# An LSTM with routed experts on one core: the first batch routed group by group, the first expert rows turned inside the last LSTM step, and scatters at most two in flight

## The reference

```python
g = xp_t + h_prev @ u                       # 512 x 512 gates, 8 steps in sequence
c = sigmoid(f) * c_prev + sigmoid(i) * tanh(cand);  h = sigmoid(o) * tanh(c)
x = layernorm(x + hs)
logits = einsum('GSM,ME->GSE', x, router_w)          # G=8 groups, S=512, M=128, E=8
# top 2 experts of a token; place p in its expert by cumulated count; kept where p < C
expert_inputs = einsum('GSEC,GSM->EGCM', dispatch, x)          # C = 128 slots
hidden = gelu(expert_inputs @ w0) * (expert_inputs @ w1)       # H = 688
out = einsum('EGCM,GSEC->GSM', hidden @ wo, combine)
y = layernorm(x + out)
```

## Time and profile before

| | |
|---|---|
| timed, median of 3 | 306.52 us |
| the profiled execution, first to last instruction | 342.1 us |
| TensorE / VectorE / ScalarE / GpSimd busy | 293.1 / 251.6 / 217.3 / 186.6 us |
| mean granted clock of TensorE | 0.921 |

### The profile page before, as it was taken

The page is one execution under the profiler, slowest core; times in us unless marked ns, Lnnn a source line. Parts: engine busy times, 40 slices in busy tenths (PEclk is TensorE's granted clock), DMA queues, the critical chain, the costliest instruction groups (busy, mean ns, idle before and its releaser), DMA issues.

```text
span 342.1 us, 5646 instructions
## 1 busy us (share of the span) xinstructions
PE 293.1 (86%) x1692; PEld 244.8 (72%) x1692; DVE 251.6 (74%) x794; ACT 217.3 (64%) x495; POOL 186.6 (55%) x153
## 2 busy tenths in 40 slices
PE   8999999697754695529999999999999999998880
PEld 6666665496744695419999987877888888888770
DVE  2789989599621585026888889889877776996985
ACT  4689887665720473026777876877765566566884
POOL 5012788887777027787773433437436536559500
PEclk9999999999885598557999999999999999999996
DMA  6996582486521015324443326344214227325265
GB/s 218 363 407 167 127 251 74 99 229 191 166 89 57 22 28 151 97 35 47 49 62 57 52 46 175 76 113 64 47 16 63 33 19 134 65 36 86 24 163 153
DMA packets 46685, 37.20 MB, mean 109 GB/s; under 512 B 7057, under 2 KB 40784, under 8 KB 46656
## 3 DMA queue, kind: packets, MB, share of 16 engines
q1 hardware_dynamic: 35392, 26.56, 26.1%
q0 software_dynamic: 11264, 10.29, 19.6%
HBM read 17.86 MB, written 17.10 MB: 102 GB/s over the span
## 4 chain that ended last, share of the span: by engine, by line
PE 67%; DVE 10%; issue 7%; ACT 6%; another core or an unknown queue 5%; POOL 3%; DMA 1%; SPq 0%; ACTq 0%; DVEq 0%
PE big L647 11%; PE big L645 11%; PE big L646 10%; PE big L552 6%; PE b_ht L664 3%; PE b_xnt L661 2%; PE b_xnt L664 2%; PE b_xnt L662 2%; PE b_ht L661 2%; PE b_ht L662 2%; PE big L538 2%; POOL tokens L494 2%; PE b_rt L681 2%; PE big L539 2%
## 5 line engine op out<-in xcount | busy, mean ns | idle before, releaser
L834 ACT ACTIVATE act_g<-big 128x256 f32<-128x256 f32 (+1 forms) x144 | 65.0, 452 | 90.8 <-PE big L647 59.6
L645 PE MATMUL big<-x_hi,e_hi 128*128 128x256 f32 (+1 forms) x264 | 89.5, 339 | 0.3 <-issue 0.3
L647 PE MATMUL big<-x_lo,e_hi 128*128 128x256 f32 (+1 forms) x264 | 86.9, 329 | 1.3 <-issue 1.3
L646 PE MATMUL big<-x_hi,e_lo 128*128 128x256 f32 (+1 forms) x264 | 86.9, 329 | 1.0 <-issue 1.0
L479 POOL DMA_INDIRECT slots<-rows,slot_ix x64 | 68.5, 1071 | 33.6 <-issue 18.5
L494 POOL DMA_INDIRECT tokens<-contrib,token_ix x32 | 51.4, 1607 | 42.2 <-DVE token_ix L1108 34.4
L494 POOL DMA_INDIRECT tokens<-zero_rows,token_ix x28 | 45.2, 1614 | 35.5 <-DVE token_ix L1108 27.5
L646 PEld LDWEIGHTS big<-x_hi,e_lo 128*128 128x128 f32 x264 | 52.9, 200 | 4.5 <-issue 1.1
L647 PEld LDWEIGHTS big<-x_lo,e_hi 128*128 128x128 f32 x264 | 52.7, 199 | 4.4 <-issue 0.4
L645 PEld LDWEIGHTS big<-x_hi,e_hi 128*128 128x128 f32 x264 | 53.0, 201 | 3.7 <-issue 0.2
L1116 DVE TENSOR_TENSOR term_i<-act_g,big 128x256 f32<-128x256 f32 (+3 forms) x36 | 18.3, 508 | 17.4 <-ACT act_g L834 12.0
(11 more groups left out here) (204 smaller groups left out, 672.9 us busy)
## 6 DMA issues: line engine op xcount, KB each, us to landing
e_raw<-in_L_ffn_w_kernel_dram SPq DMA_DIRECT2D x16, 320.0 KB
slots<-zero_rows SPq DMA_DIRECT2D x8, 548.0 KB, 7.6
e_raw<-in_L_ffn_wo_kernel_dram SPq DMA_DIRECT2D x8, 320.0 KB
xd<-slots SPq DMA_DIRECT2D x16, 137.0 KB
xd<-slots SPq DMA_DIRECT2D x8, 274.0 KB
e_lo<-e_raw POOLq DMA_DIRECT2D x4, 544.0 KB
x<-in_L_attn_input_seq_dram SPq DMA_DIRECT2D x8, 256.0 KB, 4.5
tokens<-rows SPq DMA_DIRECT2D x8, 256.0 KB
```

The source lines that it names most:

```text
L645: pe.matmul(dst, e_hi[q][:, c0:c0 + m], xdt_hi[u % 2][:, 0:w], start=True, stop=False)
L646: pe.matmul(dst, e_lo[q][:, c0:c0 + m], xdt_hi[u % 2][:, 0:w], start=False, stop=False)
L647: mm = pe.matmul(dst, e_hi[q][:, c0:c0 + m], xdt_lo[u % 2][:, 0:w], start=False, stop=True)
L834: nc.scalar.activation(act0[n % RH][0:m, 0:w], pre(n, P)[0], ACT.Gelu_apprx_tanh).then_inc(gelu_ready, 1)
```

## The change

- Batch 0 is routed as two parts, group 0 in step 2 and group 1 in step 3, each with four tiles. There are five parts r instead of four; batch 1 is routed in step 5 as before, batches 2 and 3 are parts 3 and 4. Every routing function takes a part and works on its tiles.
- GpSimd does power(0), power(1) and low_half(0,0) and then the scatters; power(2) to power(7) and three low_halfs are placed among the tiles anew: power(5) ahead of batch 1's third tile.
- From batch 2 on, each scatter from the second tile waits until the same choice's scatter of the tile before has landed (one semaphore for each choice). `load_xd` waits for both semaphores.
- `turn_xd(0)` stands behind `h_part(7)` and ahead of `turn_sum(6)`; `high_xd(0)` behind step 7's gates; on VectorE shift(5), scale_less(3), low_xd(0), stat, moment and variance of group 6 stand ahead of h of step 7. Both `keep_warm` blocks are gone.
- In units 0 and 1 turn_sum(7), places(3), logits(7), the normalizing of groups 5 to 7 and the routing of batch 2 are placed anew.

```diff
-    LOWS_AMONG = {(1, 0): (1, 0), (1, 1): (1, 1)}
-    ROOTS_AMONG = {(0, 2): 3, (0, 5): 4, (1, 0): 5, (1, 2): 6, (1, 3): 7}
+    LOWS_AMONG = {(0, 6): (0, 1), (1, 0): (1, 0), (1, 1): (1, 1)}
+    ROOTS_AMONG = {(0, 3): 2, (0, 5): 3, (0, 7): 4, (1, 2): 5, (1, 4): 6, (1, 5): 7}
+    ROUTED_IN = {2: 0, 3: 1, 5: 2}
+        def batch_of(r):
+            return max(r - 1, 0)
+        def groups_of(r):
+            return range(r, r + 1) if r < GB else range(GB * (r - 1), GB * r)
+        def tiles_of(r):
+            return slice(r * T, (r + 1) * T) if r < GB else slice(0, BT)
...
             def load_xd(u):
...
-                    sp.wait_ge(routed[b], 16 * 2 * BT)
+                    for c in range(2):
+                        sp.wait_ge(routed[b][c], 16 * BT)
...
                     for c in range(2):
+                        if b >= NB // 2 and t:
+                            pool.wait_ge(routed[b][c], 16 * t)
                         pool.indirect_dma_start(
                             slots, bass.IndirectOffsetOnAxis(ap=slot_ix[b][:, 2 * t + c:2 * t + c + 1], axis=0),
-                            rows[:, b * BT + t, :], None, bounds_check=slot_bound, oob_is_err=False).then_inc(routed[b], 16)
+                            rows[:, b * BT + t, :], None, bounds_check=slot_bound, oob_is_err=False).then_inc(routed[b][c], 16)
...
-            for s in range(3):
-                if s == 2:
-                    low_half(0, 0)
+            for s in range(2):
                 power(s)
-            low_half(0, 1)
-            for b in range(NB):
-                scatter(b, range(BT))
+            low_half(0, 0)
+            for r in range(NR):
+                scatter(r)
...
             for s in range(1, S):
                 h_part(s)
+                if s == S - 1:
+                    turn_xd(0)
                 turn_sum(s - 1)
...
-                if s >= 3 and s % 2 == 1 and s < S - 1:
-                    places(s // 2 - 1)
-            pe.wait_ge(gate_read, gate_no(S - 1, 2))
-            keep_warm(8, big[2])
-            turn_xd(0)
-            turn_sum(S - 1)
-            keep_warm(8, big[2])
+                if s in ROUTED_IN:
+                    places(ROUTED_IN[s])
...
+                    if (u, k) == (0, 3):
+                        turn_sum(S - 1)
+                    elif (u, k) == (0, 4):
+                        places(NR - 2)
+                    elif (u, k) == (0, 5):
+                        logits(S - 1)
...
+                if s == S - 1:
+                    shift(S - 3)
+                    scale_less(NR - 2)
+                    low_xd(0)
+                    stat(S - 2, range(T))
+                    moment(S - 2)
+                    variance(S - 2)
                 dve.wait_ge(tanh_ready, s + 1)
...
-            stat(S - 2, range(T))
-            moment(S - 2)
-            variance(S - 2)
-            shift(S - 3)
-            scale_less(NB - 2)
-            low_xd(0)
             for n in range(5):
-                gate_step(NB - 2, n)
-            slot_base(NB - 2)
-            void_base(NB - 2)
+                gate_step(NR - 2, n)
+            chunk(0, 0)
+            slot_base(NR - 2)
+            void_base(NR - 2)
+            chunk(0, 1)
+            shift(S - 2)
+            low_weights(2, 0)
+            chunk(0, 2)
...
```

More of the change, by code:

```diff
@@ L204, in build @@
         gate_rows_in = sem("gate_rows_in")
-        routed = [sem(f"routed{b}") for b in range(NB)]
+        routed = [[sem(f"routed{b}_{c}") for c in range(2)] for b in range(NB)]
         raw_in = [sem(f"raw_in{q}") for q in range(2)]
@@ L341, in b_xd @@
         def b_xd(u):
[L343 removed]
+            return b_xt
         def piece(n):
@@ L466, in low_half, with scatter @@
                 pool.dma_start(e_lo[e][:, cols], e_raw[e % 2][:, cols], accum_op=ALU.add).then_inc(elo_in[e], 16)
-            def scatter(b, tiles):
+            def scatter(r):
+                b = batch_of(r)
                 pool.wait_ge(zeros_out[b], 16 * GB)
-                pool.wait_ge(slot_step, AS * (b + 1))
-                pool.wait_ge(gate_rows_in, b + 1)
-                for t in tiles:
+                pool.wait_ge(slot_step, AS * (r + 1))
+                pool.wait_ge(gate_rows_in, r + 1)
+                for t in range(tiles_of(r).start, tiles_of(r).stop):
                     if (b, t) in ROOTS_AMONG:
@@ L569, in logits, with places @@
                 mm.then_inc(logits_ready, 1)
[L571 to L575, removed]
+            def places(r):
+                pe.wait_ge(chosen_ready, r + 1)
+                for g in groups_of(r):
+                    lo, pl = g % GB * T, place_ps(batch_of(r))[:, g % GB]
                     pe.matmul(pl[:, 0:T, :, :], before[:, :], chosen[:, lo:lo + T, :, :], start=True, stop=True)
@@ L743, in negative_weights, with exp @@
                 nc.scalar.activation(e_lo[e][:, piece(n)], e_hi[e][:, piece(n)], ACT.Copy, scale=-1.0).then_inc(negative_ready[e], 1)
[L745 to L747 removed]
+            def exp(r):
+                act.wait_ge(scaled, r + 1)
+                nc.scalar.activation(ex[:, tiles_of(r), :], less[:, tiles_of(r), :], ACT.Exp).then_inc(exp_ready, 1)
             def norm_rows(s, tiles):
@@ L765, in _ @@
                         high_x(1)
-                if s >= 3 and s % 2 == 1 and s < S - 1:
-                    exp(s // 2 - 1)
+                if s in ROUTED_IN:
+                    exp(ROUTED_IN[s])
+                if s == S - 1:
+                    high_xd(0)
                 for x in HIGH_X_AHEAD.get(s, []):
@@ L949, in best, with scale_less @@
                                   ALU.subtract).then_inc(less_ready, 1)
[L951 to L960, removed]
+            def scale_less(r):
+                gs, ts = groups_of(r), tiles_of(r)
+                dve.wait_ge(less_ready, gs.stop)
+                dve.wait_ge(power_ready, gs.stop)
+                view = less[:, ts, :].rearrange("p (g t) e -> p g t e", t=T)
+                q0 = gs.start % GB
+                dve.tensor_tensor(view, view, root_y[:, q0:q0 + len(gs), 0:T].unsqueeze(3).broadcast_to([P, len(gs), T, E]), ALU.mult).then_inc(scaled, 1)
@@ L1001, in assign_batch @@
                 else:
-                    dve.wait_ge(slot_step, AS * b + n)
+                    dve.wait_ge(slot_step, AS * r + n)
                 if n == 1:
-                    for g in range(GB):
+                    for g in range(gs.start, gs.stop):
                         ins = dve.tensor_tensor(place[:, g * T:(g + 1) * T, :, :], place_ps(b)[:, g, 0:T, :, :],
@@ L1186, in _ @@
             variance(S - 1)
+            chunk(0, 3)
+            assign(NR - 2, 0)
+            assign(NR - 2, 1)
             best(S - 2)
-            shift(S - 2)
-            low_weights(2, 0)
-            chunk(0, 0)
-            assign_batch(NB - 2, 0)
-            assign_batch(NB - 2, 1)
-            chunk(0, 1)
-            assign_batch(NB - 2, 2)
-            assign_batch(NB - 2, 3)
-            chunk(0, 2)
-            shift(S - 1)
-            assign_batch(NB - 2, 4)
-            assign_batch(NB - 2, 5)
-            chunk(0, 3)
-            low_weights(2, 1)
-            gate_values(NB - 2)
-            gate_row(NB - 2)
-            chunk(0, 4)
-            best(S - 1)
+            low_weights(2, 1)
+            chunk(0, 4)
+            shift(S - 1)
+            assign(NR - 2, 2)
+            assign(NR - 2, 3)
             chunk(0, 5)
             low_weights(2, 2)
-            for k in range(3):
-                chunk(1, k)
-            scale_less(NB - 1)
+            assign(NR - 2, 4)
+            assign(NR - 2, 5)
+            chunk(1, 0)
+            gate_values(NR - 2)
+            gate_row(NR - 2)
+            chunk(1, 1)
+            best(S - 1)
+            chunk(1, 2)
+            scale_less(NR - 1)
             low_weights(2, 3)
```

148 lines of the change are left out of this document (78 added, 70 removed).

## The result

The changed kernel takes 312.59 us (median of 4 runs, 311.99 to 315.27) against 306.38 us before: a ratio of 1.0226, 95% interval 1.018 to 1.0272, or 6.2 us slower. The forecast was 306.1 us, its range ended at 309.5. Medians in this document are of all runs, while a ratio and its interval leave out runs over 1.5% above the fastest of their kernel, so that a ratio need not be the quotient of the two medians beside it. The profiled execution is one of the timed ones, with a span of 310.2 us and 1.8 us around it.

What follows compares the result with a forecast made beforehand. TensorE paces the LSTM and the units from 3 on, VectorE the boundary. Sum: 306.52 - 0.3 (routing to boundary) + 0 (idle matmuls) + 0 (limit) - 0.1 (stalls) = 306.1 us; own range 305.2 to 307.2, 8 in 10 302.6 to 309.5.

Steps and rivals of the forecast that it cites:

- (b): GpSimd: first scatters near 30.1 us, xd(0) issued near 59.9, so TensorE's 2.10 us wait for the first gathered rows goes.
- the stalls of units 3 and 5: Expert units of 24.25 and 25.30 us against 6.30: 37.0 us excess, read as mostly made by profiling.
- the stall-free sum: Whole timed execution read as the profile without its stalls: span near 305.1 us (342.1 - 37.0) and 1.4 us outside.
- (a): Routing by groups in LSTM steps 2 and 3: 2.5 us more VectorE work, LSTM slip 1.6 us, bounds 0 and 2.9.
- (c): Boundary of LSTM and experts: VectorE gaps filled, new power(5) wait; net -0.96 to +0.64 us at unit 1's third chunk.
- the prediction's high bound: Start of unit 0 at half clock without the idle matmuls: +1.7 us at most, 0 taken.
- (d): Two scatters in flight: 8 us more on GpSimd, at most 12.8; +0 on time, bounds 0 and +4; stall relief -0.1.
- Who waits: Behind the limited scatters only the adds, which TensorE needs in unit 9: late by 0 to 1.5 us, 4 at most.
- the rivals: Stalls relieved, about 304.0 us (0.24); throttle makes unit 9 late, about 309.0 (0.17); boundary loses, 307.7 (0.14).

Runs made afterwards that it cites:

- e1: Changed kernel with low_half(0,1) ahead of tile 2 of batch 0 instead of tile 6: 306.86 us against 306.49 before, ratio 0.9993.
- e3: Changed kernel without the limit of two scatters in flight in batches 2 and 3: 313.03 us, ratio to before 1.022.
- e4: Changed kernel with low_half(0,1) ahead of tile 2 of batch 0 and no limit of two scatters: 305.99 us, ratio to before 0.9981.
- h2: Kernel before with only the limit of two scatters in batches 2 and 3, where before takes 306.33 us: 308.54 us, ratio 1.0108.
- h1: The kernel of e1 again on another chip: 307.01 us against 306.33 before, ratio 1.0021.
- e6: Kernel before with only the limit of two scatters in batches 2 and 3, where before takes 347.83 us: 328.67 us, ratio 0.9339.

## Why the prediction was wrong

**The step that failed** is in part (b): "now with three powers and a low_half among them". I counted low_half(0,1) as one more instruction of GpSimd, about a microsecond of its time, and asked of the power beside it who waits for it, but not of the low_half. It moved past twelve scatters, from 35.31 to 49.15 us. Its chain was all in the trace and the code of before: SyncE's load of expert 2 at 40.13, the wait of that load for both halves, and the split ahead of tanh in step 6. The prediction put this term at nothing. It measured: a load 13.9 us later, of which ScalarE waited 8.07; h_part(7) 6.8 us later than in e1 and, at half the clock, 1.7 us longer; and in the time 5.7 us (312.59 against 306.86), or 7.0 between e3 and e4, on one chip and without the limit.

**A premise that was wrong**: that the stalls of units 3 and 5 belong to the profiler, as the profiled execution was 35.6 us longer than the timed ones. The kernel before takes 348 to 351 us in its timed runs on two chips, and 306.3 to 306.5 on two others. The span of 342.1 us is like the 341.8 to 355.2 us of the stalling chips. That the first profile came from such a chip is the plain reading; the record of it does not name its chip. For the timed comparison the stall-free sum was still the right one: 305.1 us of span and 1.4 around it stand against 304.3 and 2.2 in a run of 306.49 us beside e1. (The excess of units 3 and 5 is 36.3 us and not 37.0: undisturbed, in h2, they take 6.61 and 6.63 us, not the 6.30 of unit 8.)

**The other steps**, read on e1, where the wait for the weights is out of the way:
- (a) The slip of the LSTM was put at 1.6 us, and h_part(7) at 59 to 60. A half-routing was put at 2.95 us of VectorE and takes 2.91 (1.15 + 1.76). In e1 h_part(7) starts at 59.95. Counted from h_part(1), since whole traces are shifted by up to a microsecond, h_part(6) of the changed kernel is 1.3 us later than before (39.82 against 38.52), inside the term. In e1 it is 2.8 later, and h_part(7) 2.3 later than in the profile of before and 3.0 later than in h2, just over the bound of 2.9. There low_half(0,1) stands ahead of power(2), and VectorE waits 0.94 and 0.95 us for the roots at 40.51 and 47.73: the mended place has a price of its own.
- (b) First scatter near 30.1: 30.06 in the change, 29.59 in e1. xd(0) issued near 59.9: 60.36. No wait of TensorE at turn_xd(0): none, at 63.63 (0.25 us in e4).
- (c) The wait for power(5) was put at 1 to 2.6 us and is 0.21 us in e1, where it ends at 65.14 and not at 65.5 to 67.1; power(6) has a wait of 0.94 us that I had not named. The gelu behind the two table loads was put at -0.96 to +0.64 us: it starts at 89.43 against 89.35. That agreement is partly luck, as the earlier trace rows is from a stalling run. In h2, quiet, this gelu starts at 87.80, so e1 is 1.6 us late there; at the start of unit 3 the two are level (97.48 both).
- The clock: at the start of unit 0, where the prediction's high bound had half clock, the granted clock of e1 was 1.00. It fell later: it was 0.87 on average from 73.37 to 81.66, a mix of its levels of 1.2 and 2.4 GHz, and 0.50 from 80 to 82. TensorE had been idle for 44% of the 9.37 us ahead (5.22 us busy from 64.00 to 73.37), with no matmul at all from 72 to 74. From 80 to 85 us TensorE was then busy for all of the 5.00 us at a mean of 0.72; in h2, at 1.00, for 3.90. The turn_xd(2) of e1 is 1.35 us behind h2 (84.77 against 83.42), and turn_xd(3) level (94.24 against 94.25), so what it cost was hidden by unit 3. The rows below are the first two windows of e1 (us, busy PE, PEld, DVE, ACT, POOL, clock, DMA share, GB/s), against a clock of 1.00 in the earlier trace rows. h1 repeats the fall (0.50 from 76 to 78 us). No kernel with the idle matmuls put back was run, so that their removal is the cause is not shown. The prediction's 3.1 us for a unit at 1.2 GHz is a misreading: it is the busy time of one line of three, and TensorE is busy for all of the 6.32 us of unit 8.

```profile
64.00:73.37 9.37, 5.22 (x43) 4.75 (x41) 7.43 (x30) 7.04 (x18) 8.05 (x7) 1.00 0.94 251
73.37:81.66 8.29, 5.98 (x47) 5.74 (x48) 7.99 (x43) 4.32 (x15) 6.42 (x7) 0.87 0.25 78
```

- (d) The limit costs 0 to 2.2 us on a quiet chip by the medians (e3, e1 against e4, h2), inside the bounds of 0 to +4. The value taken, 0, was right only for the change as it is, which is late enough already. On GpSimd the 32 scatters of batches 2 and 3 take 53.5 us in e1 and 42.7 in e4, so the limit adds 10.8 us, put at 8 with 12.8 as the bound. "Who waits" named only the adds and left out SyncE's load of unit 10, which is where the wait shows. By the Trainium skill ("DMA: Bandwidth & Descriptors", Anatomy of one DMA) a scatter would land in an estimated 2.16 us and the limit would be free; in e1 the median from issue to landing between 84 and 104 us is 3.0 us, and h2 shows a cost.

So with the low_half in its place the time lies in the prediction's own range of 305.2 to 307.2: 306.86 and 307.01 measured, 306.1 forecast. The small gain of it is not there (+0.4 and +0.7 us against before). None of the rivals was this one. They looked at waits that the change adds; this was an instruction that it moves.

**What stays open.** On the stalling chips TensorE and ScalarE stall while GpSimd issues indirect scatters beside expert units. A limit of two, or a slower pace, takes much of it away, four in flight do not. What the resource is, whether it is another core's work, and why two chips are free of it, no trace shows: the releaser is one that the profile does not see.

## What to carry to other kernels

- When an instruction of an in-order queue is moved, ask three things of it and not only of its neighbours: what frees a buffer or raises a semaphore with it, who issues next on that, and what stands in front of whom on the last waiter's engine. Here a DMA that costs its issuer 1 us held up a chain that ran for 14 (49.15 to 63.53).
- A wait for a transfer that stands ahead of a recurrence on a shared engine is a risk that the profile of before shows as nothing, since it is met in time. Look for its slack: the transfer's landing against the instruction's start.
- Moving such an instruction forward is not free either: ahead of power(2) the same DMA delays the roots and costs the LSTM some 1.5 us (h_part(6) 2.8 us late in e1, 1.3 in the change).
- A stall of TensorE is paid twice where the clock falls in it: 7.9 us of waiting made the next eight matmuls 1.7 us longer.
- When profile and timed runs differ by 12%, the cause is part of the question: here it was most likely the chip, and the change lost on one and won on another.

## What the runs showed of the hardware that I had not expected

The same program took 306.3 to 306.5 us on two chips and 347.8 to 350.8 us on two others. There the limit of two scatters took 17 to 19 us off the medians, a pace of 1.49 us a scatter 11.6 us, and a limit of four nothing (354.08 against 348.46). What is left under the limit is spread: in e6 unit 1 still takes 21.1 us, where h2 takes 8.7, and unit 8 takes 12.7, where h2 takes 6.3.
